# Loading the down weights and two batches of hidden values inside the last 20 beats of an attention and FFN kernel, with three down products run in the loop

## The reference, cut to what matters

```python
xn = layernorm(x)                                   # x: 4 batches x 512 rows x 512
q, k, v = split(xn @ w_qkv)                         # 16 heads of 32
q, k = rope(rmsnorm(q, q_gamma)), rope(rmsnorm(k, k_gamma))
s = softmax(causal(q @ k.T / sqrt(32))) @ v @ w_out
gate = silu(xn @ ((wq_gate - 128) * s_gate).T)      # 512 -> 1408
up   =       xn @ ((wq_up   - 128) * s_up).T
g = silu((gate * up) @ ((wq_down - 128) * s_down).T)   # 1408 -> 512
return x + s * g
```

## Time and profile before

| what | before |
|---|---|
| median of 3 runs (lowest, highest) | 750.42 us (750.28, 753.0) |
| profiled execution, its span | 753.24 us, 751.2 us |
| PE (matmul) busy | 672.3 us, 89% of the span, 3648 matmuls |
| DVE / ACT / POOL busy | 559.3 / 450.1 / 394.3 us |
| mean granted TensorE clock | 0.945 of full speed |
| DMA | 94.39 MB, mean 126 GB/s |

### The profile page before, as it was taken

One profiled execution on the slowest core, in us unless ns is written; L12 is line 12 of the kernel. 1 busy time (PEld: TensorE's weight loads), 2 busy tenths in 40 slices (PEclk: granted clock), 3 DMA queues, 4 the chain that ended last, 5 costly groups with the idle time before them and its releaser, 6 DMA issues.

```text
span 751.2 us, 12504 instructions
## 1 busy us (share of the span) xinstructions
PE 672.3 (89%) x3648; PEld 564.5 (75%) x3648; DVE 559.3 (74%) x1387; ACT 450.1 (60%) x1007; POOL 394.3 (52%) x594
## 2 busy tenths in 40 slices
PE   2579999989999999999999999999999816988996
PEld 2468887778888888788888877888888605766885
DVE  2576888998787779988877799787856838545473
ACT  2353666677676667876766688676666728423331
POOL 5443656687565657775655677756655614200000
PEclk9689999999999999999999999999999755799999
DMA  7243643524434232134343321343321191577662
GB/s 267 74 129 126 216 137 105 165 73 131 120 100 113 89 106 76 32 126 121 94 120 106 92 65 51 99 119 106 102 86 57 52 314 36 169 249 269 212 222 99
DMA packets 58994, 94.39 MB, mean 126 GB/s; under 512 B 12336, under 2 KB 15152, under 8 KB 58928
## 3 DMA queue, kind: packets, MB, share of 16 engines
q1 hardware_dynamic: 58928, 93.59, 39.6%
HBM read 59.09 MB, written 25.82 MB: 113 GB/s over the span
## 4 chain that ended last, share of the span: by engine, by line
PE 68%; POOL 8%; DVE 7%; DMA 6%; issue 5%; SPq 4%; ACT 2%; DVEq 0%; POOLq 0%; ACTq 0%
PE bank L1158 20%; PE bank L1055 14%; PE bank L1095 8%; PE bank L1174 7%; PE bank L1134 6%; PE bank L1116 5%; PE bank L1080 4%; PE bank L1067 3%; POOL rr L527 3%; POOL pp L547 2%; DMA rd_dram<-rd 1%; DVE pp L848 1%; POOL rb L536 1%; SPq L356 1%; DMA qst<-mrow 1%
## 5 line engine op out<-in xcount | busy, mean ns | idle before, releaser
L547 POOL TENSOR_SCALAR_AFFINE_SELECT pp<-pp 128x256 fp32r<-128x256 f32 x256 | 110.1, 442 | 166.5 <-DVE pp L848 166.3
L870 DVE CUSTOM_DVE_ANT_0 bank<-bank,msk_w 128x128 f32<-128x128 f32 (+3 forms) x256 | 121.2, 509 | 46.3 <-PE bank L1116 46.1
L848 DVE TENSOR_TENSOR pp<-pf,pp 128x512 fp32r<-128x512 f32 (+1 forms) x192 | 133.2, 695 | 14.6 <-ACT pp L651 14.5
L527 POOL TENSOR_TENSOR rr<-ss,half 128x8 f32<-128x8 f32 x64 | 108.4, 1694 | 46.8 <-DVE ss L816 46.7
L650 ACT ACTIVATE pf<-bank 128x512 f32<-128x512 f32 (+1 forms) x192 | 100.9, 526 | 45.1 <-PE bank L1080 36.3
L1095 PE MATMUL bank<-pp,va 128*65 128x512 f32 (+3 forms) x512 | 105.4, 327 | 9.4 <-POOL pp L547 5.2
L1158 PE MATMUL bank<-xnt_h,wgu 128*128 128x512 f32 x352 | 99.1, 403 | 4.3 <-DVE g L898 4.3
L651 ACT ACTIVATE pp<-bank 128x512 fp32r<-128x512 f32 (+1 forms) x192 | 101.1, 526 | 0.0
L1158 PE MATMUL bank<-xnt_l,wgu 128*128 128x512 f32 x352 | 96.9, 397 | 0.0
L1095 PEld LDWEIGHTS bank<-pp,va 128*65 128x65 f32 x512 | 60.9, 145 | 28.1 <-POOL pp L547 11.2
L1158 PEld LDWEIGHTS bank<-xnt_l,wgu 128*128 128x128 f32 x352 | 66.4, 189 | 16.3
(11 more groups left out here) (80 smaller groups left out, 1275.1 us busy)
## 6 DMA issues: line engine op xcount, KB each, us to landing
wgu<-wg_dram SPq DMA_DIRECT2D x66, 256.0 KB, 3.2
hf_dram<-g SPq DMA_DIRECT2D x44, 256.0 KB, 3.4
hf_raw<-hf_dram SPq DMA_DIRECT2D x44, 256.0 KB, 6.2
wg_dram<-wgu SPq DMA_DIRECT2D x22, 256.0 KB, 3.1
xr<-x SPq DMA_DIRECT2D x16, 256.0 KB, 4.5
stage<-w_gu SPq DMA_DIRECT2D x16, 256.0 KB, 3.3
oh<-oraw SPq DMA_DIRECT2D x64, 64.0 KB, 1.9
ol<-oraw SPq DMA_DIRECT2D x64, 64.0 KB, 2.0
```

Of the source, the lines that this page charges most:

```text
L527: pool.tensor_tensor(rr[:, s, :], ss[:, s, :], half[:], ALU.pow).then_inc(rr_ok, 1)
L547: op = pool.affine_select(pp[:, :, a:a + P], pp[:, :, a:a + P], [[0, 2], [1, P]], ALU.is_ge, 0.0, base=0, channel_multiplier=-1)
L848: dve.tensor_tensor(pl[:, tile], pf[:, tile], ph[:, tile].bitcast(F32), ALU.subtract).then_inc(pl_ok, 1)
L870: op = dve.tensor_tensor_reduce(bank[:, a * w:(a + 1) * w], bank[:, a * w:(a + 1) * w], msk_w[:, N - w:N], 1.0, -3.0e38, ALU.add, ALU.max, ...
```

## The change

Arithmetic and amount of work stay. Three things move.

1. **Places.** `wq_h` and `wq_l` become one tile ordered by group, `wq[P, G, 2, KT, 3*GC]`, and w_qkv and w_out are stored in DRAM so that each part of a load is one run per partition (6,144 B and 8,192 B; before four runs of 1,536 B and of 2,048 B). So groups 0 and 1 of the weights are a free stretch after projection 55, and the down weights fit there; batch 0 fits over groups 2 and 3, batch 1 over the gammas, rotation tiles and the start of `qst`.
2. **Loads and splits.** They are given out to beats by tables, below.
3. **Down products.** `down(0, 0)` is cut over beats 58 to 60, `down(0, 1)` and `down(0, 2)` stand in beats 61 and 62, and 13 stand behind the loop. The four late `out_proj` get a bank each (`LATE_PS`).

```diff
-        LOAD_AT, DOWN_AT = 57, 64
+        LOAD_WD = {45: (0, 1), 46: (2, 3), 47: (4, 5), 49: (6, 7), 50: (8, 9), 51: (10,)}
+        LOAD_HF = {53: (0, 1), 54: (2, 3), 55: (4, 5), 57: (6, 7, 8), 58: (9, 10),
+                   60: (11, 12, 13), 61: (14, 15, 16), 62: (17, 18, 19), 63: (20, 21)}
+        CAST_WD = {46: (0,), 47: (1,), 48: (2, 3), 49: (4, 5), 50: (6,), 51: (7,), 52: (8,), 53: (9,), 54: (10,)}
+        SPLIT_HF = {54: (0,), 55: (1,), 56: (2, 3), 57: (4, 5), 58: (6, 7), 59: (8, 9), 60: (10,),
+                    62: (11, 12), 63: (13, 14), 64: (15, 16, 17, 18, 19, 20, 21)}
+        DOWN_AT = {58: ((0, 0, 4),), 59: ((0, 4, 8),), 60: ((0, 8, MT),), 61: ((1, 0, MT),), 62: ((2, 0, MT),)}
...
+                for n in LOAD_HF.get(c, ()):
+                    b, m = divmod(n, MT)
+                    if b == 0:
+
+                        sp.wait_ge(qkv_full, 60 if m < 6 else NB)
+                        sp.wait_ge(hf_out[m % 2], 16 * (m // 2 + 1))
+                    else:
+
+                        sp.wait_ge(tk_full, NB)
+                        sp.wait_ge(st_full, NOP * 60)
+                        sp.wait_ge(hf_out[n % 2], 16 * (n // 2 + 1))
+                    load_hf(b, m)
...
-            for m in range(MT):
-                load_hf(1, m)
             den_in(LAST)
...
-                if c >= DOWN_AT:
-                    down(0, c - DOWN_AT)
+                for t, m0, m1 in DOWN_AT.get(c, ()):
+                    down(0, t, m0, m1)
                 if attend:
                     p_v(r, c, 0)
...
-                    wait(pe, s_ev, 4 * (B - 1) + t)
+                    if t == 1:
+                        pe.wait_ge(p_ok, NOP * NB)
+                    if t == 3:
+                        pe.wait_ge(o_ev, NB)
                     for part in range(3):
-                        out_proj(B - 1, t, part)
+                        out_proj(B - 1, t, part, LATE_PS[t])
...
-        "w_qkv": np.ascontiguousarray(ar(L0_attn_w_qkv).reshape(KT, P, 3, G, GC).transpose(1, 0, 3, 2, 4)
-                                      .reshape(P, KT, G * 3 * GC)),
+        "w_qkv": np.ascontiguousarray(ar(L0_attn_w_qkv).reshape(KT, P, 3, G, GC).transpose(1, 3, 0, 2, 4)
+                                      .reshape(P, G * KT * 3 * GC)),
```

More of the change, by code:

```diff
@@ L47 @@
 RING = 4
[L48 to L51, removed]
+AT_XR, AT_CG, AT_KST, AT_MX, AT_GU = (v // 4 for v in (65536, 128384, 161632, 194656, 211104))
+WG = 2 * KT * 3 * GC
 HALVES = 2 * MT
@@ L438, in beat @@
                     den_back((c - 5) // 4)
[L439 to L444, removed]
-                    for m in range(MT):
-                        load_wd(m)
-                        load_hf(0, m)
+                for m in LOAD_WD.get(c, ()):
+                    sp.wait_ge(qkv_full, 52 if m < 6 else 56)
+                    load_wd(m)
+                for n in LOAD_HF.get(c, ()):
[8 more added lines that the diff above has]
+                    load_hf(b, m)
             run_beats(sp, beat)
@@ L691, in high @@
                 b, m = divmod(h, MT)
+                if h == 4:
+                    act.wait_ge(gu_full, HALVES * B)
+                    act.wait_ge(qkv_full, NB)
+                if h == MT + 4:
+                    act.wait_ge(st_full, NOP * NB)
+                if b > 1 and m == 0:
+                    act.wait_ge(dn_full, 4 * (b - 1))
                 act.wait_ge(hf_in[m], 16 * (b + 1))
@@ L753, in beat @@
                     o_high(4 * r + (c - 7) // 4, G - 1)
-                for m in early_m(c):
-                    high(m)
+                for h in SPLIT_HF.get(c, ()):
+                    high(h)
             act.sem_inc(s_out[0], 16)
@@ L979, in beat @@
                 gu_weights(half_at(c + 1, 1))
-                for m in early_m(c):
+                for m in CAST_WD.get(c, ()):
                     wd_weights(m)
-                    low(m)
+                for h in SPLIT_HF.get(c, ()):
+                    low(h)
             run_beats(dve, beat)
@@ L1160, in gate_half, with down @@
                 op.then_inc(gu_full, 1)
-            def down(b, t):
+            def down(b, t, m0=0, m1=MT):
                 n = 4 * b + t
                 wait(pe, y_ok, n - 3)
[L1165 to L1170, removed]
+                if n == 0 and m0 == 0:
+                    pe.wait_ge(sq_ok, NB)
+                    pe.wait_ge(vh_ok, NB)
+                    pe.wait_ge(vl_ok, NB)
+                    pe.wait_ge(qn_ok, NB)
+                if n == 1:
+                    pe.wait_ge(hf_ok, MT * B)
+                if n == 2:
+                    pe.wait_ge(sm_ok, SM_UNIT * B * G)
+                for m in range(m0, m1):
+                    if n == 0:
+                        pe.wait_ge(wd_ok, m + 1)
                     if t == 0:
@@ L1271, in _ @@
             run_beats(pe, beat)
-            for n in range(B * 16 + 1 - DOWN_AT, B * TB):
+            for n in range(len({t for parts in DOWN_AT.values() for t, _, _ in parts}), B * TB):
                 b, t = divmod(n, TB)
```

87 lines of the change are left out of this document (44 added, 43 removed).

## The result

The changed kernel takes **741.58 us** (median of 4 runs, 739.17 to 744.26) against 750.82 for the kernel before, which ran beside it: a ratio of 0.9894, 95% interval 0.9866 to 0.9922. Measured once more, it gave 742.07 us and again 0.9894 (0.9864 to 0.9923). By the ratio it is faster by 8.0 us (the two medians lie 9.2 apart; this document goes by the ratios) and not by 20.4, and 741.58 lies outside the 722 to 740 given. The profiled execution took 742.25 us, its span is 740.1.

A forecast was written before the change was run, and what follows sets the result against it. PE was taken as the bound, except for a stall and latency chains in the late attention beats. Terms along PE put L at 636.1, PE's end at L + 88.3 = 724.4, plus 5.9: span 730.3, called 730 us, range 722 to 740.

The forecast's parts named there:

- the wait behind L: Behind the loop, PE idles some 7 us before the first late output product, which can start at L + 19.8.
- L: End of the last product with the values, 642.5 us before; the forecast's sum along PE put it at 636.1.
- The stall of 15.1 us: At beat 60, PE's wait for the maxima's store, queued behind 22 loads, goes: -15.1 us.
- L + 88.3: PE's end, at 724.4 us, after running through the late output products and the remaining down products.
- +1.1 us for beat 59: Eight down matmuls add 1.8 us, less 0.7 for the beat's start at a faster clock; bounds 0 and 3.4.
- ACT waits for loads that SP issues too late: Rival: beats 58 to 64 each bound by a load loop, some 10 us instead of 5.5; +31 us, 761; chance 0.03.
- the prediction's own signs of being wrong: Beats 61 and 62 over 9 us; output product's wait over 12 us or none; long `ht_h` load wait, beats 54 to 63.
- Beats 60 and 61: Beat 60 holds 6 down matmuls inside its latency, -0.4 us; beat 61 gets 22 and takes 6.9 us, +2.3.
- Beats 56 to 58: Four low parts on DVE in 56 and 57, +1.5 us; eight exposed down matmuls in 58, +3.4.
- Casts: Beats 46 to 55: casts and first low parts cost only where DVE becomes late; +1.0 us, bounds 0 and 2.7.
- Front: Weight loads at the start come as longer runs; only the full queue's start can move: -0.8 us, range 0 to 1.5.
- The rival of half speed in beats 60 to 62: Clock stays at half there despite the added matmuls: +1.3, +5.9 and +5.9 us, 743 in all; chance 0.12.

The follow-up runs named there:

- e2: The changed kernel with the three value loads of beat 57 issued first in SP's beat instead of last: 737.57 us, ratio 0.9851 to the kernel before.
- e5: The changed kernel with no down product in the loop and the loads of beat 57 first in SP's beat: 730.36 us, ratio 0.9748 to the kernel before.
- e3: The changed kernel with no down product in the loop, all sixteen behind it; loads, casts and splits stay: 734.0 us, ratio 0.9799 to the kernel before.
- e8: The changed kernel with two whole down products, in beats 61 and 62, loads of beat 57 first, late output products one place later: 727.05 us, ratio 0.9705.
- e6: e5 with every cast of the down weights one beat later: 728.62 us, ratio 0.9724 to the kernel before.
- e9: e8 with the casts of the down weights one beat later: 725.86 us, ratio 0.9675 to the kernel before.
- e1: The kernel before with only the attention weights stored by group, so that each load is contiguous: 747.81 us, ratio 0.9977 to the kernel before.
- e11: The changed kernel, unaltered, run and profiled once more: 742.07 us, ratio 0.9894 to the kernel before.
- e12: The kernel before, unaltered, profiled once more: 754.2 us in its one execution.
- e10: e9 with a third down product in beat 63 and the late output products one place later still: 726.35 us, ratio 0.9679 to the kernel before.

## Why the prediction was wrong

**The mechanism of the gain held, and so did the wait behind L.** The stall of 15.1 us went, and the maxima are issued at 610.75 us, right behind ACT's copy of them, which ends at 610.73. L + 19.8 for the first late output product was L + 20.9; the wait there, "some 7 us", was 8.17; PE's end at L + 88.3 was L + 90.0. Two of its terms were off and met halfway: the copy of the denominators back from DRAM was issued at L + 8.2, not L + 9.7, and the loads of x and s issued behind it landed late, so that DVE began the first result at L + 15.6, not L + 14.3. Of the 9.8 us between spans (740.1, not 730.3) 8.1 lie ahead of L and 1.7 behind it. The 8.1 are a net sum: beat 59 came 5.5 us over its term, the casts 1.6, beat 60 1.7, beat 61 1.5, beats 56 to 58 1.4 and the rest 0.5 (in it 0.2 for L before, which is 642.7 by its last product), and the front 4.1 under. Timed, the front gave 1.7 us and not the traces' 4.9, so the miss by the ratio is larger than by the spans, 12.4 us (8.0 faster where 20.4 were forecast).

**The step that failed: loads with one beat between issue and use were taken as on time,** above all those of beat 57. The sum has +1.1 us for beat 59, from 8 matmuls; it became 6.6 us longer. The wait is the one that the rival "ACT waits for loads that SP issues too late" describes, piece and beat, at a chance of 0.03 and only as a whole row of such beats. In one beat it costs 4.0 us in the trace of e2, 5.4 in that of e5, and 3.2 and 3.8 us timed. A long wait of an `ht_h` for its load was one of the prediction's own signs of being wrong, and it came; the other two, on beats 61 and 62 and on the wait before the output product, did not. The earlier trace rows had the 6.2 us to landing. A load issued at the end of SP's beat, behind a round trip to DRAM, for the very next beat of ACT, is late by about all of that; so a term of some 4 to 6 us could have been put down as an estimate. It was weighed away because "all other pieces are issued two beats ahead". That says nothing of this one, and the tables of the change contradict it: pieces 0 and 6 of the weights and 0 and 9 of the hidden values have one beat as well. The two of the weights waited too (3.28 and 1.70 us, the casts below); the two hidden pieces, first needed 8.1 us and some 10 us after their issue, did not.

**Beats 60 and 61: taken -0.4 and +2.3, real +1.3 and +3.8.** Beat 60 was said to hold six matmuls inside its latency. PE waits there 2.57 us for the low part of piece 10, split in the same beat; that this is the cause was not tested alone. Beat 61 ran its 22 matmuls in 5.95 us at a clock of 0.79, not in 5.1 at 1.00. Beat 62, at 1.00, took 7.23 against 6.9 forecast: there the sum's rule, a light beat's own 1.8 us and the matmuls, was nearly right, PE being busy 7.47 of 7.70 us. Beat 60, which it took as free, is another case: against e3 its 6 matmuls cost 1.5 us, about their own time, as the 8 of beat 58 do with 3.3, while the 22 of beat 62 cost 2.6 of their 5.1 and the rest fits into idle time. e8 shows the last two beats alone: +4.6 us for 22 matmuls, the first third of them at half clock (0.71 in the mean of the beat), and +2.7 at full clock.

**Beats 56 to 58: +6.3 instead of +4.9.** Low parts +2.2 (taken 1.5), the 8 matmuls at the pitch of half clock (0.43 us each) with the beat around them +4.1 (taken 3.4). The first is inside its bounds, the second over the 1.8 to 3.4 given.

**Casts: +1.0 taken, +2.6 in the trace** (1.9 in beat 47, 0.3 each in beats 50 and 51), inside the bound of 2.7. The cause was not DVE's work, as the sum had it, but a wait for a transfer of 8.2 us issued 5.0 us before DVE wanted it; e6 and e9 took away 1.7 and 2.2 us. The sum also counted all casts behind 500 us, while the beat that they held up most starts at 486.65.

**Front: 0.8 less taken, 1.7 less timed (0.2 to 3.3).** "A full queue ends no earlier for having fewer pieces" does not hold here: the scales landed 2.4 us earlier (POOL goes on at 19.55, not 21.99, and ahead of the 20.5 to 22 forecast), and the full queue moves more in the same time. From 12 to 18 us, before and then after:

```profile
12.00:18.00 6.00, 4.09 (x12) 3.70 (x12) 1.69 (x5) 0.63 (x3) 4.34 (x23) 1.00 1.06 379
...
12.00:18.00 6.00, 3.53 (x12) 3.02 (x10) 0.28 (x3) 0.55 (x2) 2.78 (x15) 1.00 1.03 427
```

The last column is GB/s; e1 and e11 have 425 and 427 there, e12 has 381. The Trainium skill's charge for each packet (DMA: Bandwidth & Descriptors, Why small descriptors are slow) gave 0.4 us as an estimate; the timed interval contains it, and the 0.8 too, but the traces show more: 427 against 379 GB/s is 13% more, where the 6% and 1.5% of the estimate differ by 4.5.

**The clock.** The rival of half speed in beats 60 to 62 didn't come: 0.79 in beat 61, 1.00 in 62, and 0.56 behind the gap at 660 to 665. That the gap would cost speed was in the sum with 1.6 us, measured 2.2. The Trainium skill's rule that activity releases the throttle (TensorE: Matmul & The Clock Gate, Part 1) agrees with the windows: 0.50 at 660 to 665 without a matmul, 0.56 in the next 5 us, 1.00 from 670 on.

**What was not asked at all** is what the three products are worth. The sum has them in it on one side as +7.4 us in the loop, on the other as 15.2 us less behind it, less the wait of 7 and the 1.6 at the low clock. That is a loss of 0.8 us, nothing to move work for, and it stood in the forecast's own numbers unseen. Measured it is a loss of 7.1 us (e3).

## What to carry to other kernels

Before work is moved into a stretch that looks idle, ask whether the engine's idle time there is slack or the latency of a chain; in the second case the moved work adds to it, and what it saves later is lost again if a wait of fixed length stands behind it. Cost a moved product together with its alternative, here "loads early, products late" (e3), which took the stall out and was 7 us better. And for each early load set its issue in the queue against the first need, one by one: two hidden pieces needed one beat after loads that stood behind a round trip, and casts one beat too soon, cost some 3 and 2 us.

## What the runs showed of the hardware

A load of 256 KB took 6.3 to 8.2 us to landing where it was late, also in stretches that look quiet on average. The first load of the down weights took 8.2 us in a window whose mean is 92 GB/s (440 to 500), but while it was under way the engines were full:

```profile
480.15:488.40 8.25, 8.25 (x49) 6.98 (x48) 3.59 (x12) 5.05 (x13) 2.94 (x7) 1.00 0.98 262
```

So a load's time is to be read beside the traffic of its own few us (DMA share 0.98, 262 GB/s), not beside the mean of a stage. The order in which the attention weights are stored changed the rate of a full queue from 379 to 427 GB/s. The front varies by up to 3.8 us from one execution to the next with the same instructions up to there (beat 0 at 68.42 after and 72.22 in e10), while from beat 0 to beat 47 all traces of this study take 417.9 to 418.8 us. Behind that the beats that wait for a load vary again: beat 47 takes 11.05 to 13.47 us in the traces with the early casts. A single profile compares fronts badly and waits for loads to a us or two, and the rest well.
